# Attention in two halves of 64 tokens: early queries leave out late keys, context in eight 64x32 tiles

## The reference

```python
c = einsum('bsi,boi->bso', x, cond_weight[ids_a])        # a 512x512 weight for each batch
q, k, v = rope(c @ Wq), rope(c @ Wk), c @ Wv
scores = where(causal, -inf, einsum('bgptd,bgsd->bgpts', q, k))
x1 = x + softmax(scores / 4) @ v @ Wo
y = x1 @ W.T + (x1 @ lora_A[ids_b]) @ lora_B.T * 0.5
w = onehot(top2(y @ W_router.T)) * softmax(top2)
out = x1 + y @ W_base.T + b_base + experts(y, w) * 2
```

## Time and profile before

| | us |
|---|---|
| runs | 246.1, 246.0, 247.74 |
| median of the runs | 246.1 |
| profiled execution, its span | 244.0 |
| PE busy | 230.3 (94%) |
| DVE busy | 182.1 (75%) |
| ACT busy | 121.5 (50%) |
| POOL busy | 96.9 (40%) |

### The profile page before, as it was taken

One profiled execution on the slowest core, in us unless ns is written; L12 is line 12 of the kernel. 1 busy time (PEld: TensorE's weight loads), 2 busy tenths in 40 slices (PEclk: granted clock), 3 DMA queues, 4 the chain that ended last, 5 costly groups with the idle time before them and its releaser, 6 DMA issues.

```text
span 244.0 us, 5779 instructions
## 1 busy us (share of the span) xinstructions
PE 230.3 (94%) x2010; PEld 175.3 (72%) x2010; DVE 182.1 (75%) x903; ACT 121.5 (50%) x271; POOL 96.9 (40%) x108
## 2 busy tenths in 40 slices
PE   6899998989899999999999999999999998999893
PEld 6688975766578677867777777777777774556793
DVE  2789357538966996699659965997599769949663
ACT  3687435577276256716671667166712660254010
POOL 7300572468269125912592249224932320002120
PEclk9999999999999999999999999999999999999999
DMA  5999308015002610161016101710100110003011
GB/s 134 339 378 349 151 6 266 1 18 201 12 3 50 212 51 6 43 218 45 11 47 215 45 13 46 215 45 13 43 3 25 33 43 3 0 3 89 10 46 43
DMA packets 20049, 21.18 MB, mean 87 GB/s; under 512 B 6452, under 2 KB 11572, under 8 KB 20020
## 3 DMA queue, kind: packets, MB, share of 16 engines
q1 hardware_dynamic: 20020, 20.81, 27.0%
HBM read 18.71 MB, written 2.10 MB: 85 GB/s over the span
## 4 chain that ended last, share of the span: by engine, by line
PE 74%; DVE 15%; issue 3%; ACT 3%; DMA 2%; SPq 1%; POOL 1%; DVEq 0%; ACTq 0%
PE bank L1030 12%; PE bank L1035 11%; PE bank L1031 10%; PE bank L1091 5%; PE bank L1118 5%; DVE thrown L725 5%; PE bank L1041 4%; PE bank L1057 4%; PE bank L1132 3%; PE bank L1134 3%; PE bank L1133 3%; PE bank L1084 2%; DMA stage_d<-base_t 2%; PE bank L1098 2%; PE bank L1267 2%
## 5 line engine op out<-in xcount | busy, mean ns | idle before, releaser
L725 DVE CUSTOM_DVE_ANT_0 thrown<-bank,causal 128x128 f32<-128x128 f32 x256 | 56.2, 287 | 0.2
L359 POOL TENSOR_TENSOR cond_w_lo<-cond_raw,cond_w_hi 128x512 fp32r<-128x512 f32 x28 | 35.3, 1289 | 22.8 <-ACT cond_w_hi L442 22.8
L379 POOL TENSOR_TENSOR rope_b<-rope_a,rope_b 128x128 f32<-128x128 f32 (+1 forms) x16 | 16.3, 1018 | 38.1 <-DVE rope_b L777 38.1
L442 ACT ACTIVATE max_rows<-bank,own_p 128x128 fp32r<-128x128 f32 x32 | 9.1, 370 | 26.0 <-PE bank L1067 26.0
L388 POOL TENSOR_TENSOR x_bias<-x,bias_row 128x512 f32<-128x512 f32 x8 | 10.2, 1280 | 29.8 <-DVE out_sb L898 28.4
L1030 PE MATMUL bank<-qkv_w_hi,c_t_hi 128*128 128x512 f32 (+1 forms) x64 | 21.3, 350 | 0.6 <-DVE c_t_lo L662 0.5
L725 DVE DVE_READ_ACCUMULATOR2_ANT neg_max<- 128x1 f32 x256 | 21.4, 84 | 0.0
L1030 PE MATMUL bank<-fused_w_hi,late 128*128 128x324 f32 (+2 forms) x68 | 21.2, 325 | 0.0
L1031 PE MATMUL bank<-qkv_w_lo,c_t_hi 128*128 128x512 f32 (+1 forms) x64 | 20.5, 337 | 0.0
L1031 PE MATMUL bank<-fused_w_lo,late 128*128 128x324 f32 (+2 forms) x68 | 19.9, 306 | 0.0
L400 POOL TENSOR_TENSOR out_sb<-stage_b,x_bias 128x324 f32<-128x324 f32 x5 | 4.4, 883 | 37.0 <-ACT stage_b L442 37.0
(11 more groups left out here) (163 smaller groups left out, 642.5 us busy)
## 6 DMA issues: line engine op xcount, KB each, us to landing
cond_raw<-cond_w_t SPq DMA_DIRECT2D x7, 1024.0 KB, 5.6
xt_raw<-x_t SPq DMA_DIRECT2D x8, 256.0 KB, 5.9
x_nat<-x SPq DMA_DIRECT2D x8, 256.0 KB, 2.7
out<-out_sb SPq DMA_DIRECT2D x8, 256.0 KB, 2.2
stage_d<-base_t SPq DMA_DIRECT2D x4, 256.0 KB, 4.5
cond_raw<-cond_w_t SPq DMA_DIRECT2D x4, 256.0 KB, 4.3
stage_b<-w SPq DMA_DIRECT2D x4, 256.0 KB, 5.3
stage_a<-w_q SPq DMA_DIRECT2D x4, 256.0 KB, 5.4
```

Of the source, the lines that this page charges most:

```text
L359: pool.tensor_tensor(cond_w.lo[:, k, :], cond_raw[:, k, :], f32(cond_w.hi[:, k, :]), ALU.subtract).then_inc(cond_lo, 1)
L379: pool.tensor_tensor(qk[:, at:at + w], rope_a[:, at:at + w], rope_b[:, at:at + w], ALU.add).then_inc(qk_ready, 1)
L442: return nc.scalar.activation(out, in_, ACT.Copy, scale=scale)
L725: nc.vector.tensor_tensor_reduce(thrown[:, p % 2, j, e, :], s_ps[j][:, at:at + P], causal[:, :], -1.0, -MASKED, ALU.add, ALU.min, neg_max[ ...
```

## The change

The 128 tokens of a batch are cut into an early and a late half of 64. q, k and the exponentials are laid out by half (`q_t` as half, head, token; `k_pad` as half, group of a pair, token).
- Score blocks are now b = 0 to 3: two for early queries (two heads each, 128 columns: only the early keys) and two for late queries (256 columns). DVE's maxima of blocks 0 and 1 read 64 elements a row in place of 128. Block 2 is computed with 0 and 1 at the end of the round before; block 3 stays in the round, behind the context, and waits for the maxima of blocks 0 to 2.
- `score_t(t, h)` is by key half: h = 0 for early keys, 512 columns (all queries), h = 1 for late keys, 256 columns (late queries only). The mask is now two groups of four 32x128 tiles of 256 columns, after the passes.
- `context(r)` is one block of 16 calls: for each half four pairs by two groups, each a 64x32 tile; h = 0 has 512 columns and h = 1 256.
- The order of every engine changes around it.

The core of the diff, PE first:

```diff
+            def mask_t(t, h):
+                for u in range(2):
+                    for j in range(PAIRS):
+                        nc.tensor.matmul(s_ps[j][:, 0:2 * P],
+                                         after[tile_rows(j), u, :, :].rearrange("p e s -> p (e s)"),
+                                         here[tile_rows(j), u, :].unsqueeze(1).broadcast_to([TILE, PER, HALF_T]),
                                          start=False, stop=False)
...
+                for h in range(2):
+                    for j in range(PAIRS):
+                        pe.wait_ge(exped, 8 * r + PAIRS * h + j + 1)
+                        for e in range(2):
+                            mm = nc.tensor.matmul(ctx_ps(r, e)[tile_rows(j), D - score_width[h]:D],
+                                                  v_ones[r % 2][h][half_rows(e), j, :, :],
+                                                  probs_t[h][j][half_rows(e), :], start=(h == 0), stop=(h == 1))
                 mm.then_inc(ctx_done, 1)
...
             def project_kv_high(f):
                 if f > 1:
                     pe.wait_ge(ctx_turned, 2 * (f - 1))
...
             score(0, 1)
+            score(0, 2)
             condition(1)
             transpose_c(1)
-            score(0, 2)
             score(0, 3)
+            project_kv(1)
             project_q(1)
-            project_kv(1)
...
+                condition(f, range(2))
                 if batch(q):
                     transpose_hidden(q)
+                condition(f, range(2, KT))
+                transpose_c(f)
+                context(r)
+                score(t, 3)
+                project_q_high(f)
                 if batch(q):
                     finish_ffn(q)
+                project_q_low(f)
+                project_kv_high(f)
+                transpose_maxima(t)
+                project_kv_low(f)
+                passes_t(t, 0)
+                mask_t(t, 0)
+                less_maxima(t, 0)
+                project_out(r)
+                passes_t(t, 1)
+                mask_t(t, 1)
+                less_maxima(t, 1)
+                transpose_x1(r)
+                transpose_qk(f)
+                ffn_high(r, 0, left_ps(r), ks=range(KT // 2))
+                project_low(r)
+                ffn_high(r, 0, left_ps(r), ks=range(KT // 2, KT))
+                ffn_low_half(r, 0, left_ps(r))
+                ffn_rank(r, 0, left_ps(r)).then_inc(gates_done, 1)
+                if f < LAST:
+                    ffn_high(r, 1, right_ps(r))
+                    ffn_low_half(r, 1, right_ps(r))
+                score(f, 0)
+                score(f, 1)
+                score(f, 2)
+                if f < LAST:
+                    ffn_rank(r, 1, right_ps(r))
```

DVE, with its wait of a score block, its calls in t = 0 and in a round:

```diff
+                dve.wait_ge(scored, PER * t + max(b + 1, PER - 1))
...
             maxima(0, 1)
             split_c(1)
+            split_fused(7)
             maxima(0, 2)
             maxima(0, 3)
...
+                split_c(f)
+                turn_context(r, 0)
+                maxima(t, 3)
+                split_maxima(t)
+                scale_context(r, 0)
+                turn_context(r, 1)
+                scale_context(r, 1)
+                turn_back(r)
+                rotate_k(f)
+                rotate_q(f)
+                split_context(r)
+                add_x(r)
+                split_x1(r)
+                split_k(f)
+                split_low(r)
+                split_q(f)
```

ACT splits xt(0) ahead of the rank weights at the start, and in a round splits a(r) and then xt(g) behind the four quarters of the condition weight, ahead of the spreading of the maxima; x1 now comes ahead of k. POOL, at the start and in a round:

```diff
+            split_xt(0)
             tables()
-            split_xt(0)
...
+                if prep and t > 1:
+                    split_condition(g, 0)
+                    split_xt(g)
+                    split_condition(g, 1)
+                    split_condition(g, 2)
+                    split_a(r)
+                if batch(q):
+                    add_bias(q)
+                add_rotated(f, rope_q, 0, D)
+                add_rotated(f, rope_k, D, KV)
```

More of the change, by code:

```diff
@@ L123, in build_program @@
         own_max = sb("own_max", [P, 2])
-        pick_max = [sb(f"pick_max{e}", [P, P], F32R) for e in range(2)]
+        pick_max = sb("pick_max", [P, 2, HALF_T], F32R)
         rope_cos = sb("rope_cos", [P, HD])
@@ L439, in _ @@
+            add_bias(LAST - 2)
+            split_a(LAST - 1)
+            add_bias(LAST - 1)
+            split_a(LAST)
+            add_bias(LAST)
         @block.scalar
@@ L611, in _ @@
                 f, r, q, g = t + 1, t - 1, t - 2, t + 2
-                prep = batch(f) and batch(g)
                 if batch(q):
@@ L1120, in context, with condition @@
                 mm.then_inc(ctx_done, 1)
-            def condition(f):
+            def condition(f, ks=range(KT)):
                 pe.wait_ge(xt_hi, f + 1)
                 pe.wait_ge(xt_lo, f + 1)
-                if f > 0:
+                if f > 0 and ks[0] == 0:
                     pe.wait_ge(q_lo, f)
-                for k in range(KT):
+                for k in ks:
                     if f == 0:
@@ L1353, in _ @@
-                if batch(r):
-                    ffn_high(r, 0, left_ps(r), ks=range(KT // 2))
-                    project_low(r)
-                    ffn_high(r, 0, left_ps(r), ks=range(KT // 2, KT))
-                    ffn_low(r, 0, left_ps(r)).then_inc(gates_done, 1)
-                if batch(f):
-                    score(f, 0)
-                    score(f, 1)
-                if batch(r) and f < LAST:
-                    project_ffn(r, 1, right_ps(r))
-            context(LAST - 1, 0)
```

489 lines of the change are left out of this document (224 added, 265 removed).

## The result

The changed kernel takes 272.0 us (median of five runs, 271.7 to 275.0) against 246.1: a ratio of 1.106, interval 1.101 to 1.111. It is slower, as forecast, but by 25.9 us and not by 12, and it lies 3 us above the range. The profiled execution has a span of 273.1 us and is the slowest of the five (275.0); a median run is 3 us shorter.

What follows compares the result with a forecast made beforehand. PE was taken as the bound, without slack, at 24.70 us a round. 244.0 + 4.2 (start) + 6 x (2.0 waits - 2.07 saved) = 247.8; + 8.0 (DVE stalled by POOL) + 2.1 (profile to median) = 258 us; range 250 to 269.

Steps and rivals of the forecast that it cites:

- PE work removed in a round: PE's saving per round from context, late half of transposed scores and fewer tile-shape changes: 2.07 us.
- the start: From the first matmul through t = 0: later warm-up and first score, wait for maxima, less some savings: net 4.2 us slower.
- The context's .40: Context block on PE: late-key half has half the columns, eight 64-row tiles side by side, saving .40 us a round.
- the late half's .47: Late half of the transposed scores on PE: four groups at half the columns, saving .47 us a round.
- The six changes of tile shape: PE's round: 9 changes of tile shape in place of 15, at .2 us each, saving 1.2 us.
- Waits in a round: New PE waits at four places in each round: 2.0 us in sum, between .7 and 3.2.
- The copy's .69: PE's transposes of c, right behind the condition, wait for ACT's copy to `turn`: .7 us taken a round.
- k's .38: `project_low` on PE waits for the split of k: .8 us taken a round.
- The lock: POOL's moved block stalls DVE's cast, subtraction and scalings in t = 2 to 5: 2.0 us each, 8.0 in all.
- Rival B: Granted clock falls behind PE's waits at t = 0 and in rounds: 2.9 us a fall, 264 to 270 us, chance .17.
- A: The forecast itself as a case for the whole kernel: 254 to 263 us, chance .48.
- the wait of 3.7: At t = 0 `score(0, 3)` waits 3.7 us for maxima DVE takes up behind its splits of c(1) and fused weights.

Runs made afterwards that it cites:

- e8: Changed kernel with POOL's whole round ordered as in the kernel before (bias, base and output, split of a, rotations, then low parts): 260.3 us.
- e9: e8 plus the start's tables as before, block 2's maxima at t = 0 ahead of the splits, x1's split earlier in the tail: 252.8 us.
- e12: e11 with a batch's last five feed-forward matmuls moved into the next round, between the condition and the transposes of c: 245.1 us, ratio .994.
- e4: Changed kernel with 14 matmuls, results thrown away, ahead of the K/V projection in t = 2 to 6: 270.5 us, ratio 1.099.
- e11: e9 with DVE splitting the transposed hidden ahead of the maxima of block 2: 248.1 us, ratio 1.007.

## Why the prediction was right and wrong

The step that failed first is the PE work removed in a round: the prediction's sum has 2.07 us, the profiles show .65. Beside it, the sum has no term for the falls of the clock and too small a one for the start.

By medians: the changed kernel lost 25.9 us. POOL's order in the rounds, with the three falls behind its waits, is 11.7 of them (272.0 to 260.3, e8); the start and t = 0 are 7.5 (260.3 to 252.8, e9, whose edit of the tail gained nothing); the rounds' other waits, PE's small gain and the tail are 6.7 (252.8 to 246.1). The prediction had 8.0, 4.2 and 0, together 12.

**PE work removed: wrong, the largest miss.** I summed 2.07 a round; PE's busy time fell by .65, in the changed kernel and in e12 alike. The 1.4 that did not come are 8.5 us over six rounds. The context's .40 came (.53 with what the two blocks saved at their edges: 1.98 to 1.45), and so did the late half's .47. The six changes of tile shape at .2 each, 1.2 in all, did not: about .5 came. The early half of the transposed scores shows why. PE before, from the mask to the output projection:
```profile
141.67 0.43 PE L1084 MATMUL bank<-later_b,ident_b 32*32 32x512 bf16 x16
142.03 0.50 PE L1091 MATMUL bank<-q_t_hi,k_pad_hi 32*128 32x512 f32 x4
...
142.83 0.41 PE L1098 MATMUL bank<-max_rows,pick_max 32*128 32x512 f32 x4
143.17 0.50 PE L1030 MATMUL bank<-shared,late 128*128 128x512 f32 x1
```
and in the changed kernel:
```profile
105.61 0.50 PE L1097 MATMUL bank<-q_t_hi,k_pad_hi 32*128 32x512 f32 x4
...
106.42 0.40 PE L1105 MATMUL bank<-here,after 32*128 32x256 bf16 x8
106.57 0.49 PE L1115 MATMUL bank<-max_rows,pick_max 32*128 32x512 f32 x4
107.07 0.48 PE L1044 MATMUL bank<-shared,late 128*128 128x512 f32 x1
```
The mask went from .36 to .15, but the matmuls that subtract the maxima, behind it, from .34 to .50; the whole took 1.50 before and takes 1.46. The late half gained .60, .13 more than its columns; the context's edges are another .13, and finishing the experts, which now stands inside the q projection, went from .95 to .75. And what the regrouping splits costs something, by e12, where no long wait blurs it: the q projection, which the experts now cut in two, and the K/V projection take 3.1 + 1.7 in place of 2.9 + 1.6, the feed-forward about .3 more, and smaller pieces together as much again. I had taken a price from one kind of place and multiplied it by a count over other kinds, and had not counted the boundaries that the new order opens.

**Waits in a round: right in kind, one missing.** The copy's .69 and k's .38 were there; x1's was .23 at t = 1 and less after that. The wait ahead of the context for the hidden (.6) showed only once POOL's order was mended, and I had not named it: the change moved the hidden's split behind three blocks of maxima (two before), and the context behind it. Without the saving to pay for them, these waits make t = 2 to 5 longer by 25.9 - 24.7 = 1.2 us each. Together that is 4.7 of the 8.0 us by which e9's profiled span (252.0) exceeds the one before (244.0); t = 1 is as long as before (25.3), t = 6 with the tail adds 2.5 and the start .7.

**The lock: right.** Place, rounds and instructions are those forecast: .80 of idle at t = 1, none at t = 6, 2.45 to 2.62 at t = 2 to 5, against 2.0 plus .2. Four instructions in a row were hit, of which three stand ahead of the turn; against e8 these three lost .60, 1.03 and .82, together the 2.45 of the idle. What the lock cost in the end is less: at full clock the rounds t = 2 to 5 take 111.3 us in e4 and 103.6 in e8, 7.6 more, against 8.0 forecast, because e8 has the wait for the hidden in place of it. The Trainium skill ("SBUF — State Buffer", section "Who interferes with whom") says that whichever of DVE and GpSimd issues first holds the shared ports for its whole instruction while the other stands still. The rows agree for the cast and the subtraction, which end .03 and .08 behind POOL's instruction; the scalings end .3 behind it. So did the scaling of the earlier trace rows (62.17 against 61.88), of which I wrote that it ends when POOL's does.

**The clock: right in mechanism, wrong in weight.** Rival B had a chance of .17 and the forecast none of its price. In fact it came on top of A: six falls in the profiled execution, two of them at the start, three in the rounds at 1.4 us each. They belonged behind the waits I had forecast, as a term of the sum (half of them, say) and not as a rival beside it. I had taken 2.9 us a fall from the warm-up, though no row shows the lower level there: the granted clock of the kernel before reads 1.00 from 2 to 8 us. The stretches in the rounds cost half of that. Nor is .85 the longest wait of the kernel before once its start is over, as I wrote: it has two of 1.02 and 1.07 (at 66.77 and 205.86), with a full clock behind both.

**The start: 4.2 forecast, 7.5 measured.** The late warm-up and the wait of 3.7 (3.51) at t = 0 were right. But the first score came 5.5 later, where I had 2.9 and at most 3.8. Missed were DVE's tables, which the diff moves behind the first rotation and whose casts then meet POOL (1.96 us), and the two falls of the clock behind these waits. The tail, which I set at nothing because it has the same pieces regrouped, has a wait of 2.32 with a fall behind it; from the start of t = 6 on the changed kernel takes 66.6 us, against 64.9 before.

**The range** was too narrow upward because A and B were treated as alternatives: 264 to 270 for B came from A plus two to four falls, with PE's gain of 2.07 still in the sum. Without the part of that gain that did not come (1.4 a round, six times) B reads 272 to 279, at a price of a fall that was twice too high; that the measured 272.0 is its lower end is luck.

## What to carry to other kernels

Where PE has no slack, price the work saved at the very places that change, and count the boundaries that a regrouping opens as well as those it closes; a saving that is one count times one price is a guess. A wait of some microseconds on PE is to be priced with the fall of the clock that may follow it, in the sum itself. And a call that moves on a side engine takes its dependences along: of three ways to move POOL's block back, two turned its cost into a new wait on POOL (for one bias of 1.25 us and for one split of .46), and only the third left none.

## What the runs showed of the hardware

A change of tile shape has no fixed price: about .2 us at the score blocks before, but six fewer a round brought about .5 and not 1.2. Eight 64x32 tiles run side by side (.86 us for eight calls of 512 columns, .59 for eight of 256). Narrowing a row-tiled group from 256 to 128 columns bought nothing (24 matmuls in .72 and .71). A DVE cast of 128x32, .18 by itself, took .78 behind one POOL instruction, and one of 128x128 took 1.29. A fall of the clock is no sure consequence of a wait: e11 has two short ones at t = 0 (.69 and .50, at 38.68 and 40.75) and then half the clock from 41 to 44.5 us; the kernel before has the same two and a full clock behind them. And filling an idle stretch of 2.6 us with matmuls whose results nobody reads saved 1.4 us in each round in which the clock would have fallen, and cost 2 us in t = 6, where there was nothing to fill.
